# Layer 1 of a CIN network as three fp32r terms, with the low parts of the squares on GpSimd, and a rearranged front and last pair

## The chip, the cores and the metric

One core of a Trainium2 chip. The metric is the device time of one execution in microseconds (us). Each timed run gives one time; the kernel before took 430.91 us in the median of three (430.17 to 431.34).

## The reference

The model is an xDeepFM recommender with a batch of 512, 26 features, an embedding width of 32 and 13 dense values, all in float32:

```
emb  = tables[feature, sparse]                        # 512 x 26 x 32
for w, b in ((conv1_w, conv1_b), (conv2_w, conv2_b)): # two CIN layers
    hp = einsum('bhd,bmd->bhmd', xk, x0)              # x0 = emb; xk = emb, then 64 rows of layer 1
    xn = sigmoid(einsum('oi,bid->bod', w, hp) + b)    # 128 outputs
    xk, res = xn[:, :64], res + xn[:, 64:]
cin_out  = sum over the width of res, times cin_w, + cin_b
deep_out = 832+13 -> 1024 -> 512 -> 256 -> 1 with tanh on emb and dense
out = linear(sparse, dense) + cin_out + deep_out + bias   # 512 values
```

## The kernel before

The batch is cut into 16 *pairs* of 32 rows; a pair has two halves c of 16 rows times 32 embedding columns, so 512 columns each. The order of every engine is written out by hand; engines meet at semaphores that only count up.

**Layer 1 by squares.** Since 2ab = (a+b)² - a² - b², the products of all feature pairs come from squares. TensorE adds rows in `sums_of` (L396 to L405; `x` is stored as an fp32r high part and an fp32r low part), ScalarE squares the 351 sums into `sq` (`squares`, L562), in 3 tiles of 117, and `layer1` (L407) multiplies them by the weights `w1_sb` in plain fp32: 3 tiles u, two column halves q, so 6 matmuls a half c and 12 a pair. fp32 matmuls appear in the trace as two instructions each. The two column halves run side by side in the array. `sigmoid` (L571) makes `xk` and `res1` of the result.

**Layer 2 by products.** For each of 13 tiles t of a pair VectorE multiplies `xk` by a repeated row of x0 (L730), and `main` (L435) multiplies the product by `w2_sb` in fp32. Seven of the tiles take the repeated row from PSUM, where `spread_tile` (L423) puts it by an fp32r matmul into a ring of three double banks shared with the sums (`slot_free`, L386); six ("copied", tiles 2, 3, 6, 7, 10, 11) take it from SBUF, where SyncE's broadcasts put it (L305, 256 KB each and two a tile). `sigmoid2` (L584) and `fold2_of` end the layer.

**Order in the loop.** TensorE's order in pair i is in L507 to L520: four groups of tiles, before each the sums and spreads listed for it (`SUMS_IN`, `SPREADS_IN`), behind the first two `layer1(i + 1, c)`. VectorE (L716 to L746) runs the 13 products, with `x_low(i + 2)` (L659, two subtractions of 0.68 us) behind t = 5, `fold1_of`, `turn` (a transpose for the deep part), `fold2_of` and `piece_low` (low part of a piece of the weights W1) between. GpSimd issues the gathers of embedding rows (L347), seven a pair, one pair after the other, each when the one before has landed. SyncE lays gathered rows out in HBM (`lay_out`), brings them back (`fetch`, into `raw`) and issues the broadcasts; `fetch(i + 3)` is the last thing of its iteration i, behind six broadcasts that wait for `main_done`. ScalarE rounds `raw` to `x` (`x_high`, L552).

**The deep part.** Three layers with fp32r terms hi·hi, lo·hi and hi·lo (`deep`, L448). W1 comes in 14 pieces, one a pair, which ScalarE and VectorE split; the input `xt` is split in the last pair by ScalarE (L640) and GpSimd (L376), and `deep(0, 0)` stands in the last pair behind tile 7. After layer 0, TensorE adds the dense part (L537) and the CIN sums (L541) into the row of outputs; the last tanh, two fp32 matmuls (L545), one addition on VectorE and one DMA end the kernel.

**The front.** 13 fp32 matmuls (L476) keep TensorE busy until pair 0 has come; then sums, layer 1 and spreads of pair 0. `x_low(1)` stands behind VectorE's second product.

## Time and profile before

| What | Time, us |
|---|---|
| Timed runs, median (lowest to highest) | 430.91 (430.17 to 431.34) |
| The profiled execution, own time | 432.29 |
| Span of its trace | 430.4 |
| TensorE busy | 413.3 |
| VectorE busy | 320.0 |
| GpSimd busy | 167.3 |
| ScalarE busy | 161.0 |

The span runs from the first to the last instruction; what lies outside it, 1.9 us of the profiled execution's own time, is start and end of the launch. Busy times are sums over the span, and matmuls are pipelined: a matmul's own time is longer than the distance to the next one, so costs on TensorE are read from starts. A wait is told with the instruction that ended it.

### The profile page before, as it was taken

How to read it: one execution, taken by the hardware profiler on the slowest of the kernel's cores; microseconds unless marked ns; L12 is line 12 of the kernel's file. 1: busy time of each engine (PE TensorE's matmuls, PEld its weight loads, DVE VectorE, ACT ScalarE, POOL GpSimd, SP SyncE). 2: the span in 40 equal slices, each digit the busy share in tenths (PEclk: the TensorE clock that was granted, in tenths of full speed). 3: DMA queues.
4: the chain of work that ended last, by engine and by line, in shares of the span. 5: the costliest groups of instructions: out<-in, count | busy, mean ns of one | idle time of the engine just before them, and what ended most of it. 6: DMA issues, size and time to landing. Idle time of an engine off the chain costs nothing. (4 is left out here: it accounts for less than half of the span.)

```text
span 430.4 us, 5216 instructions
## 1 busy us (share of the span) xinstructions
PE 413.3 (96%) x1874; PEld 167.6 (39%) x1874; DVE 320.0 (74%) x356; ACT 161.0 (37%) x264; POOL 167.3 (39%) x146
## 2 busy tenths in 40 slices
PE   3978989999999999999999999999999999999997
PEld 1422323333333333333233333333333344886784
DVE  4115799898999799999798998998989895332121
ACT  3073252544544534535253544443543411111011
POOL 6663466664746584675540000000000193870000
PEclk9996999999999999999999999999999999999999
DMA  5357696888786898778887778675856720320000
GB/s 195 82 122 164 168 229 162 194 192 196 177 202 141 200 193 210 173 191 184 191 190 189 178 186 192 163 201 133 213 143 153 177 66 10 114 76 0 0 2 0
DMA packets 38304, 64.03 MB, mean 149 GB/s; under 512 B 19601, under 2 KB 22033, under 8 KB 38278
## 3 DMA queue, kind: packets, MB, share of 16 engines
q1 hardware_dynamic: 34694, 61.93, 58.3%
q0 software_dynamic: 3584, 1.76, 3.3%
q8 instruction: 15, 0.25, 0.2%
q14 instruction: 11, 0.09, 0.1%
HBM read 61.96 MB, written 1.71 MB: 148 GB/s over the span
## 5 line engine op out<-in xcount | busy, mean ns | idle before, releaser
L355 POOL DMA_INDIRECT emb<-in_table,rows x112 | 132.8, 1186 | 86.1 <-DMA emb<-in_table,rows 52.6
L730 DVE TENSOR_TENSOR prod<-ring,xk 128x1024 f32<-128x1024 f32 x112 | 132.7, 1217 | 29.2 <-PE ring L431 14.2
L730 DVE TENSOR_TENSOR copied<-copied,xk 128x1024 f32<-128x1024 f32 x96 | 115.4, 1242 | 0.5
L441 PE MATMUL conv<-prod,w_sb 128*64 128x512 f32 x448 | 112.2, 615 | 0.0
L441 PE MATMUL conv<-copied,w_sb 128*64 128x512 f32 x384 | 91.9, 594 | 1.5 <-DVE copied L730 1.5
L419 PE MATMUL conv<-sq,w_sb 117*64 117x512 f32 x384 | 88.1, 593 | 0.3 <-issue 0.3
L579 ACT ACTIVATE xk<-conv,const_sb 64x512 f32<-64x512 f32 x64 | 43.7, 683 | 97.2 <-PE conv L419 84.1
L376 POOL TENSOR_TENSOR xt_lo<-xt,xt_hi 128x512 fp32r<-128x512 f32 (+1 forms) x7 | 12.8, 1863 | 122.1 <-ACT xt_hi L640 122.1
L568 ACT ACTIVATE sq<-ring 117x512 f32<-117x512 f32 x90 | 48.6, 594 | 29.7 <-PE ring L403 23.5
L441 PEld LDWEIGHTS conv<-copied,w_sb 128*64 128x64 f32 x384 | 26.8, 137 | 57.6 <-issue 45.4
L419 PEld LDWEIGHTS conv<-sq,w_sb 117*64 117x64 f32 x384 | 27.2, 136 | 54.2 <-issue 53.4
L441 PEld LDWEIGHTS conv<-prod,w_sb 128*64 128x64 f32 x448 | 26.7, 137 | 50.1 <-issue 45.7
L431 PE MATMUL ring<-x,sel_sb 58*128 58x512 f32 x224 | 39.4, 414 | 0.7 <-ACT sq L568 0.7
L664 DVE TENSOR_TENSOR x<-raw,x 26x512 fp32r<-26x512 f32 x32 | 21.9, 683 | 23.8 <-ACT x L559 21.4
L559 ACT ACTIVATE x<-raw 96x512 fp32r<-96x512 f32 x16 | 10.1, 631 | 53.5 <-DMA raw<-laid 50.0
L403 PE MATMUL ring<-x,sel_sb 58*117 58x512 f32 x96 | 24.3, 497 | 4.7 <-issue 4.7
L431 PEld LDWEIGHTS ring<-x,sel_sb 58*128 58x128 f32 x224 | 19.6, 185 | 22.1 <-issue 16.6
L403 PEld LDWEIGHTS ring<-x,sel_sb 58*117 58x117 f32 x96 | 9.0, 180 | 43.3 <-issue 39.9
L760 DVE CAST h_hi<-hf 128x512 fp32r<-128x512 f32 x8 | 7.7, 964 | 20.7 <-ACT hf L652 20.6
L581 ACT ACTIVATE res<-conv,const_sb 64x512 f32<-64x512 f32 x32 | 21.9, 685 | 0.8
L589 ACT ACTIVATE res<-conv,const_sb 128x512 f32<-128x512 f32 x16 | 11.1, 691 | 22.1 <-PE conv L441 21.5
L760 DVE CAST xt_hi<-hf 128x512 fp32r<-128x512 f32 x4 | 1.7, 427 | 20.1 <-ACT hf L652 20.1
(76 smaller groups left out, 299.2 us busy)
## 6 DMA issues: line engine op xcount, KB each, us to landing
copied<-laid SPq DMA_DIRECT2D x192, 256.0 KB
wpiece<-in_mlp SPq DMA_DIRECT2D x22, 256.0 KB
emb<-in_table,rows POOLq DMA_INDIRECT x112
raw<-laid SPq DMA_DIRECT2D x32, 52.0 KB
laid<-emb SPq DMA_DIRECT2D x16, 96.0 KB
sel_f<-in_sel SPq DMA_DIRECT2D x1, 832.0 KB, 5.7
const_sb<-in_const SPq DMA_DIRECT2D x1, 626.0 KB, 4.2
w_sb<-in_w SPq DMA_DIRECT2D x1, 416.0 KB, 6.3
```

Of the source, the lines that this page charges most:

```text
L355: pool.indirect_dma_start(out=emb[0:n, i, j, :], out_offset=None, in_=table, in_offset=bass.IndirectOffsetOnAxis(ap=rows[0:n, i, j:j + 1], ...
L376: nc.gpsimd.tensor_tensor(xt_lo[0:n, k, :], xt[0:n, k, :], xt_hi[0:n, k, :].bitcast(F32), ALU.subtract).then_inc(xt_lo_done, 1)
L403: mm = nc.tensor.matmul(sums_bank(i, u)[0:UK, c, :], sel1_sb[at:at + XK, u, :], x[i % RX][at:at + XK, :], start=True, stop=True)
L419: mm = nc.tensor.matmul(l1_bank(i, c)[o, :], w1_sb[:, u, o], sq[i % 2][0:UK, u, c, :], start=(u == 0), stop=(u == UT - 1))
L431: mm = nc.tensor.matmul(spread_bank(r)[:, c, :], sel2_sb[at:at + XK, t, :], x[i % RX][at:at + XK, :], start=True, stop=True)
L441: mm = nc.tensor.matmul(conv[i % 2][c * HALF:(c + 1) * HALF, :], w2_sb[:, t, :], prod_of(r)[:, c, :], start=(t == 0), stop=(t == T2 - 1))
L568: nc.scalar.activation(sq[i % 2][0:UK, u, c, :], sums_bank(i, u)[0:UK, c, :], ACT.Square)\
L579: nc.scalar.activation(xk[i % 2][q * HALF:(q + 1) * HALF, c, :], bank[0:HALF, :], ACT.Sigmoid, bias=small_sb[0:HALF, C_CB1:C_CB1 + 1]).the ...
L581: nc.scalar.activation(res1[i % 2][c * HALF:(c + 1) * HALF, :], bank[HALF:P, :], ACT.Sigmoid, bias=small_sb[HALF:P, C_CB1:C_CB1 + 1]).then ...
L589: nc.scalar.activation(res2[i % 2][:, :], conv[i % 2][:, :], ACT.Sigmoid, bias=small_sb[:, C_CB2:C_CB2 + 1]).then_inc(l2_read, 1)
L664: nc.vector.tensor_tensor(x[i % RX][at + XLO:at + XK, :], raw[i % RX][at:at + M, :], x[i % RX][at:at + M, :].bitcast(F32), ALU.subtract).t ...
L730: nc.vector.tensor_tensor(prod_of(r)[:, :, :].rearrange("p c n -> p (c n)"), left[:, :, :].rearrange("p c n -> p (c n)"), xk[i % 2][:, :, ...
```

## The change

1. **Layer 1** for pairs 2 to 15: ScalarE, behind each two squares, also writes their rounded copies `sq_hi`; the low part `sq - sq_hi` is made per (u, c), five of six on GpSimd (`LOWS`) and (2, 0) on VectorE behind its tile 2. `layer1` issues 18 fp32r matmuls of full width (128 columns) a pair instead of 12 fp32 ones of half width. Pairs 0 and 1 keep fp32.
2. **GpSimd's order**: in pair i it waits for product 4, 8 and 12, does one, two and two low parts, and then three, two and two gathers of pair i + 4. Only the first four pairs are gathered ahead of the loop. `gather(1)` no longer waits for the rows of pair 0.
3. **TensorE's groups** are tiles 0-3, 4-7, 8-10, 11-12. The sums of pair i + 2 now stand behind groups 0 and 1, in front of `layer1(i + 1, c)`, and in front of group 2.
4. **The low part of x**: four fetches a pair instead of two (raw also lands in the rows of the low part), one instruction on VectorE instead of two, behind tile 2 instead of 5. `fetch` stands in front of the fifth broadcast of its iteration, `lay_out` behind the second. `x_high(i + 2)` is the first thing of ScalarE's iteration.
5. **Front**: 12 warm matmuls instead of 13; the dense part's fp32 matmul and a copy on ScalarE stand in pair 0; `x_high(1)` stands ahead of `sigmoid(0, 1)`, `x_low(1)` ahead of the first product.
6. **W1**: the low parts of its last 5 of 7 row tiles are made in the last two pairs, in room that the squares leave (`late_copy`, `late_low`, `late_high`); VectorE splits only 4 pieces in the loop. `xt` is split up to its last 32 columns from pair 14 on, the rest in pair 15. `deep(0, 0)` stands behind tile 10.
7. **End**: the CIN sums are weighed on VectorE and need one fp32 matmul after layer 0; the last tile of the last deep layer, its tanh, the row matmul and the addition are cut in halves of 256 columns.

```diff
-LAY_AT = 3
-DEEP_AT = 1
-GROUPS = ((0, 1, 2, 3), (4, 5, 6, 7), (8, 9, 10, 11), (12,))
+LAY_AT, FETCH_AT = 1, 4
+DEEP_AT = 2
+GROUPS = ((0, 1, 2, 3), (4, 5, 6, 7), (8, 9, 10), (11, 12))
-SUMS_IN = {0: ((1, 2),), 2: ((2, 0),), 3: ((2, 1),)}
+SUMS_BEFORE = {2: ((2, 2),)}
+SUMS_BEHIND = {0: ((2, 0),), 1: ((2, 1),)}
-X_LOW_AT, TURN_AT, FOLD1_AT, PIECE_AT = (10, 5), 9, (5, 7), 11
-WARM = 13
+X_LOW_AT, TURN_AT, FOLD1_AT, PIECE_AT = (10, 2), 9, (5, 5), 11
+KEEP = 2
+LOW_AT, LATE_AT = 2, 10
+WARM = 12
@@ tensor, layer1(i, c) for i >= 2
-                for u in range(UT):
-                    pe.wait_ge(sq_done, squares_up_to(i, u, c))
-                    for q in range(2):
-                        o = slice(q * HALF, (q + 1) * HALF)
-                        mm = nc.tensor.matmul(l1_bank(i, c)[o, :], w1_sb[:, u, o], sq[i % 2][0:UK, u, c, :],
-                                              start=(u == 0), stop=(u == UT - 1))
+                for u in range(UT):
+                    pe.wait_ge(sq_hi_done, highs_up_to(i, u, c))
+                    nc.tensor.matmul(bank[:, :], w1_hi[:, u, :], sq_hi[i % 2][0:UK, u, c, :],
+                                     start=(u == 0), stop=False)
+                    nc.tensor.matmul(bank[:, :], w1_lo[:, u, :], sq_hi[i % 2][0:UK, u, c, :],
+                                     start=False, stop=False)
+                for u in range(UT):
+                    if (u, c) in LOWS:
+                        pe.wait_ge(sq_lo_done, lows_up_to(i, u, c))
+                    else:
+                        pe.wait_ge(sq_lo_dve, i - 1)
+                    mm = nc.tensor.matmul(bank[:, :], w1_hi[:, u, :], sq_lo[i % 2][0:UK, u, c, :],
+                                          start=False, stop=(u == UT - 1))
@@ scalar, squares(i, u)
+                if i >= 2:
+                    for c in range(2):
+                        act.wait_ge(sq_done, squares_up_to(i, u, c))
+                        nc.scalar.activation(sq_hi[i % 2][0:UK, u, c, :], sq[i % 2][0:UK, u, c, :], ACT.Copy)\
+                          .then_inc(sq_hi_done, 1)
@@ gpsimd
+            def sq_low(i, u, c):
+                pool.wait_ge(sq_hi_done, highs_up_to(i, u, c))
+                nc.gpsimd.tensor_tensor(sq_lo[i % 2][0:UK, u, c, :], sq[i % 2][0:UK, u, c, :],
+                                        sq_hi[i % 2][0:UK, u, c, :].bitcast(F32), ALU.subtract)\
+                  .then_inc(sq_lo_done, 1)
...
+            for i in range(GSEM):
+                gather(i)
             for i in range(NPAIR):
-                gather(i)
+                ahead = i + GSEM < NPAIR
+                pool.wait_ge(prod_done, T2 * i + 4)
+                if 2 <= i + 1 < NPAIR:
+                    sq_low(i + 1, 2, 1)
...
+                if ahead:
+                    gather(i + GSEM, range(0, 3))
+                pool.wait_ge(prod_done, T2 * i + 8)
+                if 1 <= i and i + 2 < NPAIR:
+                    sq_low(i + 2, 0, 0)
+                    sq_low(i + 2, 0, 1)
...
+                if ahead:
+                    gather(i + GSEM, range(3, 5))
+                pool.wait_ge(prod_done, T2 * i + 12)
...
+                if i + 2 < NPAIR:
+                    sq_low(i + 2, 1, 0)
+                    sq_low(i + 2, 1, 1)
...
+                if ahead:
+                    gather(i + GSEM, range(5, GJ))
@@ vector, x_low(i)
-                for c in range(2):
-                    at = HALF * c
-                    nc.vector.tensor_tensor(x[i % RX][at + XLO:at + XK, :], raw[i % RX][at:at + M, :],
-                                            x[i % RX][at:at + M, :].bitcast(F32), ALU.subtract).then_inc(x_lo_done, 1)
+                nc.vector.scalar_tensor_tensor(x[i % RX][0:XEND, :], raw[i % RX][0:XEND, :],
+                                               small_sb[0:XEND, C_LOW:C_LOW + 1],
+                                               x[i % RX][0:XEND, :].bitcast(F32),
+                                               ALU.mult, ALU.subtract).then_inc(x_lo_done, 1)
@@ tensor, end of layer 0
-                    nc.tensor.matmul(row_ps[0:1, :], small_sb[:, C_AUX:C_AUX + 1], aux[:, :], start=True, stop=False)
-                    by_c = row_ps[0:1, :].rearrange("p (i c b) -> p c i b", c=2, b=CB)
-                    for k, col in enumerate((C_CIN1, C_CIN2)):
-                        for c in range(2):
-                            nc.tensor.matmul(by_c[:, c], small_sb[:, col + c:col + c + 1],
-                                             fold[:, k, :, :], start=False, stop=False, skip_group_check=True)
+                    pe.wait_ge(cin_step, 2)
+                    nc.tensor.matmul(cin_ps, small_sb[:, C_ONE:C_ONE + 2], fold[:, 0, :, :], start=True, stop=True)\
+                      .then_inc(cin_done, 1)
```

## Rows read from the trace of the kernel before

**Rows 1.** the page: busy us; granted clock in 40 slices, in tenths

```profile
PE 413.3 (96%) x1874; PEld 167.6 (39%) x1874; DVE 320.0 (74%) x356; ACT 161.0 (37%) x264; POOL 167.3 (39%) x146
...
PEclk9996999999999999999999999999999999999999
```

**Rows 2.** a 20 us stretch of the loop: busy by engine

```profile
140.00:160.00 20.00, 20.00 (x98) 6.34 (x96) 17.82 (x20) 9.09 (x15) 13.19 (x11) 1.00 0.91 196
```

**Rows 3.** waits of TensorE: us in total, times, longest

```profile
PE conv L441 <- DVE copied L730: 1.5, 3, 0.7
```

**Rows 4.** timeline of TensorE in the loop: start us, us, what

```profile
63.76 1.89 PE L441 MATMUL conv<-copied,w_sb 128*64 128x512 f32 x8
65.47 2.75 PE L419 MATMUL conv<-sq,w_sb 117*64 117x512 f32 x12
...
205.92 2.75 PE L419 MATMUL conv<-sq,w_sb 117*64 117x512 f32 x12
208.60 0.72 PE L431 MATMUL ring<-x,sel_sb 58*128 58x512 f32 x4
...
326.62 1.89 PE L419 MATMUL conv<-sq,w_sb 117*64 117x512 f32 x8
```

**Rows 5.** the chain that ended last: start us, us, what

```profile
367.29 4.78 PE conv L462 x21
...
395.97 0.95 PE conv L537 x2
396.92 1.73 PE conv L541 x8
...
423.58 2.76 PE ring L462 x12
426.34 1.82 PE conv L545 x4
...
428.18 0.68 DVE row_sb L767
```

**Rows 6.** timeline of one pair: a fetch, its landing, who waits

```profile
201.61 0.91 SPq L294 DMA_DIRECT2D raw<-laid  x2
...
207.99 0.63 ACT L559 ACTIVATE x<-raw 96x512 fp32r<-96x512 f32 x1 [4.65 <-DMA raw<-laid]
...
208.65 1.40 DVE L664 TENSOR_TENSOR x<-raw,x 26x512 fp32r<-26x512 f32 x2 [2.23 <-ACT x L559]
```

**Rows 7.** groups of instructions: busy us, mean ns | idle before, releasers

```profile
L730 DVE TENSOR_TENSOR prod<-ring,xk 128x1024 f32<-128x1024 f32 x112 | 132.7, 1217 | 29.2 <-PE ring L431 14.2 <-ACT xk L579 9.5 <-PE conv L441 2.9
L355 POOL DMA_INDIRECT emb<-in_table,rows x112 | 132.8, 1186 | 86.1 <-DMA emb<-in_table,rows 52.6 <-issue 31.4 <-DVE rows L701 2.1
L664 DVE TENSOR_TENSOR x<-raw,x 26x512 fp32r<-26x512 f32 x32 | 21.9, 683 | 23.8 <-ACT x L559 21.4 <-issue 1.7
L365 POOL TENSOR_TENSOR m_lo<-wpiece,m_hi 128x512 fp32r<-128x512 f32 x10 | 13.2, 1319 | 0.8
```

**Rows 8.** VectorE's products: duration min, median, max ns

```profile
L730 DVE TENSOR_TENSOR prod<-ring,xk x112: 1205/1216/1227, 31.1 to 357.5; 128x1024 f32<-128x1024 f32 x112
L730 DVE TENSOR_TENSOR copied<-copied,xk x96: 1178/1218/2319, 34.9 to 354.8; 128x1024 f32<-128x1024 f32 x96
```

**Rows 9.** timelines of GpSimd and then VectorE in the last pair

```profile
343.23 12.83 POOL L376 TENSOR_TENSOR xt_lo<-xt,xt_hi 128x512 fp32r<-128x512 f32 x7 [122.09 <-ACT xt_hi L640]
...
346.59 3.55 DVE L730 TENSOR_TENSOR copied<-copied,xk 128x1024 f32<-128x1024 f32 x2
```

**Rows 10.** timelines of the first pair, TensorE and then VectorE

```profile
26.83 2.79 PE L419 MATMUL conv<-sq,w_sb 117*64 117x512 f32 x12
34.30 1.40 PE L403 MATMUL ring<-x,sel_sb 58*117 58x512 f32 x2 [4.68 <-issue]
...
38.24 1.97 PE L441 MATMUL conv<-prod,w_sb 128*64 128x512 f32 x4
...
42.26 1.23 DVE L730 TENSOR_TENSOR prod<-ring,xk 128x1024 f32<-128x1024 f32 x1 [5.00 <-PE ring L431]
```

More of the change, by code:

```diff
@@ L38 @@
 GSEM = 4
+XEND = HALF + XK
 RING = 3
@@ L256, in build @@
                     enter(("spread", r))
+                for j, u in sums_of_group(SUMS_BEHIND, i, g):
+                    enter(("sums", j, u))
         def l1_bank(i, c):
@@ L720, in _ @@
                     if t == 0:
+                        if i == 0:
+                            x_low(1)
                         dve.wait_ge(xk_ready, 4 * (i + 1))
```

351 lines of the change are left out of this document (264 added, 87 removed).

## The prediction

> **What bounds the kernel now.** I read the page's totals and clock line first, then one stretch of the loop, the waits of TensorE, its timeline, the chain that ended last, and last the groups and the places where GpSimd meets VectorE. TensorE is busy for 96% of the span at full clock but for the start and a dent early on [rows 1]. In 20 us of the loop it is busy for all 20.00, VectorE for 17.82, GpSimd for 13.19, and the DMA engines for 0.91 of their time [rows 2]. In the whole kernel TensorE waits for VectorE's copied products for 1.5 us [rows 3]. So TensorE's own work sets the pace of the loop, VectorE has 2.2 us of slack in 20, and the DMA engines have not much either. The period is read from TensorE's timeline: the first half of layer 1 of pair 2 starts at 65.47 and that of pair 15 at 326.62 [rows 4], so 261.15 / 13 = 20.09 us a pair. Behind the loop the chain is TensorE alone up to the last 0.68 us on VectorE [rows 5].
>
> **Layer 1 (change 1, on the path).** A half of layer 1 now runs from 205.92 to the next kind of work at 208.60, 2.68 us [rows 4]; two halves make 5.36 us a pair. The trace has no fp32r layer 1, but fp32r matmuls of full width in the deep part: 21 of them in 4.78 us [rows 5], 0.228 us each, partly with 77 rows, so the 117 rows here should cost the same. 18 x 0.228 = 4.10 us. Equal fp32 steps are 0.43 us apart (four from 63.76 to 65.47), so six would be 2.57; the last, into fp32r, is 0.1 us longer. That doesn't go, it moves to the sums in front, and 2 x 0.1 us come back. Saved: 5.36 - 4.10 - 0.20 = 1.06 us a pair, x 14 pairs = 14.8 us. From below: if the weight loads can't all be hidden, nothing is saved; from above, 1.26 x 14 = 17.6 us. I take 14.8, since weight loads of the same size are hidden in those 21.
>
> **ScalarE and VectorE (off the path).** ScalarE gets six copies of 117x512 a pair, by the 0.63 us of its rounding of x [rows 6] 3.8 us; its busy time is 9.09 of 20 us [rows 2], so it goes to about 12.9 in 19. VectorE loses one of two subtractions of 0.68 us in x_low and, from pair 5 on, a piece_low (taken at the same 0.68), and gains one sq_low (0.68): 17.8 - 0.7 = 17.1 us a pair in 19. Both are hidden, VectorE with 1.9 us to spare.
>
> **GpSimd (change 2).** A subtraction takes 1.32 us there (L365), a gather 1.19 us and 0.3 us to the next (31.4 us of "issue" over some 100 of them) [rows 7]. 5 x 1.32 + 7 x 1.49 = 17.0 us a pair in 19: it fits if nothing holds it. The question is what it does to VectorE. Products that read PSUM take 1.205 to 1.227 us whatever else runs; copied ones, which read SBUF twice, take 1.218 but once 2.319 [rows 8]. That was in the last pair, where GpSimd's seven subtractions took 12.83 us, 1.83 each instead of 1.32, and two copied products 3.55 us instead of 2.35 [rows 9]. So they hold each other up, by 1.1 to 1.2 us at a time for VectorE and 0.5 for GpSimd. The change starts the low parts when product 4, 8 or 12 is done. Behind 4 and 8 stand two products from PSUM (2.3 us), behind 12 three (3.4 us); one low takes 1.3, two take 2.6. The first and third place hold them; the second overlaps by 0.3 us with the transpose and the reduction behind product 9, which read one tile each. I take no collision as the rule. Between that and one collision for each low (5 x 1.17 = 5.9 us on VectorE) lies the range. The gathers fall beside copied products as before, where those kept 1.218 us; I take them at nothing. If they slip, their cover is the pair in which a gather is ahead of its lay_out.
>
> The page "SBUF — State Buffer" of the Trainium skill (section "Who interferes with whom") says that a VectorE instruction with two SBUF inputs shuts out a GpSimd instruction that reads SBUF and the other way round, while one with a single SBUF input does not. The trace agrees, with 2.319 against 1.227 us. By that rule it is the place of each low part that decides, which is my second rival.
>
> **Fetches and order (changes 3, 4).** raw is asked for at 201.61 and has landed at 207.99, and VectorE stands 2.23 us for it [rows 6], though TensorE loses only some tenths by that. The new fetch goes out one group of tiles (about 3.5 us) earlier, but is wanted at tile 2 instead of 5, some 5 us of VectorE's order earlier; four issues instead of two cost SyncE 0.9 us more, beside 12 broadcasts a pair. I cost it at nothing; if it comes late, x_low stops VectorE ahead of product 3. The sums of u = 2 now stand right before the spreads that need their bank: the spread of the next tile 1 waits for ScalarE's two squares, which stand behind three sigmoids. And from that spread to product 3 VectorE has three products, x_low and sq_low (about 3 x 1.14 + 1.3 = 4.7 us, with semaphores 5.2), while TensorE has two mains, the next spreads and three mains (about 5.4 us). That is close; I take 0.2 us a pair as lost, -2.8 us in 14 (bounds: +0.4 a pair, when today's small waits go too, and -1.0). New period: 20.09 - 1.06 + 0.20 = 19.2 us.
>
> **Front (change 5).** Now TensorE stands from about 29.6 to 34.30 (4.68 us idle), its granted clock falls to the 1.2 GHz level (the dent in [rows 1]), one tile of main takes 1.97 us, and VectorE waits 5.00 us for the spread of tile 4, until 42.26 [rows 10]. With x_high(1) and x_low(1) first, the sums of pair 1 can start near 31.5 and product 0 about 0.7 us later than now. If the clock holds at 2.4 GHz, tile 4 starts near 37.5, 4.8 us earlier; if it falls all the same, near 40, 2.5 us earlier. Product 0 can also come 1.5 us late. I take 4.0 us (bounds 1 to 5.5). The dropped warm matmul pays for the moved dense one.
>
> **Last pair and end (changes 6, 7).** In the last pair the same work stands in another order: deep(0, 0) waits for ScalarE's and GpSimd's splits either way and is now covered by fewer mains, but GpSimd has started earlier. 0, bounds -2 and +1.5. Behind layer 0, 0.95 + 1.73 = 2.68 us [rows 5] become one matmul of 256 columns and the steps into it, about 0.75 us: +1.9. The end: 24 matmuls of 256 columns for 12 of 2.76 us [rows 5]; I take +0.4 us for their 24 weight loads (bounds 0 and +2.7, half-width ones no faster than the 0.228 us of whole ones). Halved, the last tanh (some 0.6 us), row matmul (half of 1.82) and addition (0.68) give back about 0.2 + 0.4 + 0.3 = 0.9. Together 1.9 + 0.9 - 0.4 = 2.4 us saved.
>
> The page "TensorE: Matmul & The Clock Gate" of the Trainium skill (section "LDWEIGHTS (loading the stationary operand)") gives a load of 128 columns 128 / 1.2 = 107 ns, as long as 256 columns at full clock. No run here shows such a pair yet. By that page's figure the halves cost nothing and the estimate for the end would be 2.8 us.
>
> **Sum.** 14.8 - 2.8 + 4.0 + 0 + 2.4 = 18.4 us. Against the profiled execution's own 432.29 us: 413.9. The median of the runs shown is 1.4 us lower, so 412.5 us.
>
> **Rivals.**
> 1. *All goes well.* The clock holds in the front, today's waits go, the end saves all: 14 x 0.4 more, 1.5 and 0.5: about 405 us. For it: TensorE's waits are small now. Against it: the close race before product 3. Chance 0.13.
> 2. *VectorE takes over.* With n collisions of 1.17 us a pair its work is 17.1 + 1.17 n. From n = 2 it passes TensorE's 19.0 (19.4, and what the rings add, say 19.8): 14 x 0.6 = 8.4 us back, 421 us. For it: GpSimd's places have 0 to 0.8 us of spare, and a low part that waits for ScalarE's copy starts late. Against it: VectorE's slack of 1.9 us takes one. Chance 0.20.
> 3. *The DMAs come late.* At a share of 0.91 in 20 us the same bytes in 19.2 us make 0.95, and raw's landing (6.4 us) grows. If VectorE stands 0.5 to 1 us a pair for x_low, 7 to 14 us are back: 420 to 427 us. Against it: the share falls to two thirds once gathers are over, and a part of W1's work moves. Chance 0.10.
> 4. *GpSimd falls behind (the other side).* At 1.83 us a low part its pair is 5 x 1.83 + 7 x 1.49 = 19.6 us, over the period; then each place starts late, lows meet copied products again and layer 1 waits for `sq_lo`. With n = 3, VectorE's pair is 20.6 and with 4 it is 21.8: 14 x (20.6 - 19.2) = 20 us and 36 us above the forecast, 432 to 449 us. It is slower than before from n = 3 on. Against it: it needs most places missed, and from pair 12 on there are no gathers. Chance 0.12.
>
> **Chances and range.** The forecast has 0.45. Faster by over 0.3%, about 1.3 us, which is what a measurement of this kernel can tell: the forecast, rivals 1 and 2 and most of 3, 0.86. Within 0.3%: the far end of 3 and the near end of 4, 0.03. Slower: the rest of 4, 0.11. The range that leaves out 2 in 10 goes from 404 to 425 us.
>
> **What would show it.** Starts of layer 1's matmuls 0.228 us apart and a period of 19.2 us between its blocks; all "prod" products at 1.22 us and no copied one near 2.3; GpSimd's low parts at 1.3 us, not 1.8; tile 4 of pair 0 before 40 us and TensorE's clock at full there; TensorE's waits in the loop under 0.3 us a pair. The forecast is wrong if VectorE's copied products lengthen by the dozen, if VectorE waits for x in most pairs, or if TensorE waits for low parts on GpSimd.

## The result: 1.3% slower, where 4% faster was forecast

The changed kernel takes 436.48 us (median of 4 runs, 435.37 to 438.35), the kernel before 431.12 us beside it. The ratio is 1.0133, 95% interval 1.0094 to 1.0172. The forecast was 412.5 us with a range of 404 to 425.

The traces are of one execution each. For the changed kernel that is its fastest, 435.37 us, and for the kernel before one of 432.29: 3.1 us apart, where the medians are 5.4 apart. What follows places the 3.1 (2.8 in their spans); the other 2.3 lie between executions, and no trace shows them.

The page of the changed kernel: busy time by engine, TensorE's granted clock in tenths in 40 slices, then VectorE's two groups of products (busy us, mean ns).

```profile
span 433.2 us, 5332 instructions
PE 410.3 (95%) x1798; PEld 190.8 (44%) x1798; DVE 337.4 (78%) x357; ACT 214.2 (49%) x363; POOL 258.2 (60%) x221
...
PEclk9986996999999999999999999999999999999999
...
L954 DVE TENSOR_TENSOR prod<-ring,xk 128x1024 f32<-128x1024 f32 x112 | 132.4, 1215 | 17.7 <-PE ring L576 16.5
L954 DVE TENSOR_TENSOR copied<-copied,xk 128x1024 f32<-128x1024 f32 x96 | 134.8, 1431 | 0.0
```

TensorE's work fell by only 3.0 us (413.3 in [rows 1]). The clock line has a second dent now (a stretch at 1.2 GHz), in the seventh slice, and the slice ahead of the first is lower too. In the trace the granted clock is at 1.2 GHz from 24.1 to 27.5, from 34.3 to 41.2 and from 68.5 to 75.3 us; before, only from 33.7 to 40.5. Copied products take 1.431 us on average, where their median was 1.218 [rows 8]; the others still take 1.215.

To place the difference I cut every trace at the start of VectorE's first product of a pair. All times are us of the profiled execution. The last columns are the span and the median with its ratio to the kernel before. Dents come on top in some traces: the rest of 91.9 us in e4, e9 and e17 holds one of 3.4 us near the end of the loop. The traced execution of e3 took 437.37 us, 1.9 over its median; that of e11 took 433.66, 2.4 under.

| kernel | first product | pair 0 | pair 1 | pairs 2-14, mean | rest | span | median | ratio |
|---|---|---|---|---|---|---|---|---|
| before | 31.1 | 27.7 | 18.7 | 20.04 | 92.4 | 430.4 | | 1 |
| changed | 34.1 | 24.1 | 27.1 | 19.82 | 90.3 | 433.2 | 436.48 | 1.0133 |
| e1 | 35.0 | 23.3 | 26.6 | 20.59 | 90.7 | 443.2 | 444.19 | 1.0308 |
| e2 | 33.7 | 25.5 | 25.1 | 19.72 | 90.4 | 431.1 | 433.21 | 1.0053 |
| e3 | 34.4 | 23.8 | 26.3 | 20.03 | 90.4 | 435.3 | 435.45 | 1.0106 |
| e4 | 34.2 | 23.2 | 28.4 | 20.03 | 91.9 | 438.1 | 439.08 | 1.0171 |
| e5 | 33.6 | 23.5 | 27.8 | 21.54 | 90.3 | 455.1 | 456.80 | 1.0606 |
| e6 | 31.6 | 26.6 | 24.2 | 19.77 | 90.4 | 429.8 | 432.35 | 1.0043 |
| e7 | 33.7 | 23.8 | 23.0 | 19.75 | 90.3 | 427.5 | 428.76 | 0.9947 |
| e8 | 32.0 | 26.5 | 18.7 | 20.10 | 90.1 | 428.6 | 429.21 | 0.9963 |
| e9 | 31.9 | 26.8 | 26.6 | 19.75 | 91.9 | 433.9 | 434.41 | 1.0045 |
| e10 | 32.1 | 25.2 | 28.5 | 19.68 | 90.3 | 432.0 | 432.50 | 1.0016 |
| e11 | 35.2 | 24.4 | 23.8 | 19.46 | 95.1 | 431.5 | 436.03 | 1.0056 |
| e12 | 30.6 | 26.5 | 20.6 | 20.56 | 92.4 | 437.2 | 439.35 | 1.0169 |
| e13 | 32.7 | 25.6 | 24.4 | 19.71 | 90.3 | 429.3 | 430.80 | 0.9977 |
| e14 | 33.8 | 23.2 | 26.3 | 19.83 | 90.3 | 431.5 | 431.09 | 0.9985 |
| e15 | 34.0 | 23.8 | 23.8 | 19.85 | 90.4 | 430.0 | 432.75 | 1.0024 |
| e16 | 33.8 | 24.3 | 20.9 | 19.67 | 90.3 | 425.0 | 427.47 | 0.9930 |
| e17 | 34.1 | 23.7 | 20.6 | 19.63 | 91.9 | 425.5 | 426.29 | 0.9892 |

The changed kernel against before: front and pair 0 together -0.6 us (+3.0 and -3.6), pair 1 +8.4, pairs 2 to 14 -0.22 each, -2.8 in all, the rest -2.1. That makes +2.9, and the spans differ by 2.8. So two questions stand: why layer 1 gave so little, and what happened in pair 1.

**Layer 1.** TensorE's timeline in the changed kernel (start us, us, what; x8 counts the instructions of a row):

```profile
157.72 1.89 PE L586 MATMUL conv<-copied,w_sb 128*64 128x512 f32 x8
159.53 0.49 PE L529 MATMUL ring<-x,sel_sb 58*117 58x512 f32 x2
159.95 0.50 PE L555 MATMUL conv<-sq_hi,w_hi 117*128 117x512 f32 x1
160.29 0.39 PE L557 MATMUL conv<-sq_hi,w_lo 117*128 117x512 f32 x1
160.51 0.39 PE L555 MATMUL conv<-sq_hi,w_hi 117*128 117x512 f32 x1
...
161.43 0.84 PE L564 MATMUL conv<-sq_lo,w_hi 117*128 117x512 f32 x3
162.20 0.49 PE L529 MATMUL ring<-x,sel_sb 58*117 58x512 f32 x2
162.53 0.63 PE L576 MATMUL ring<-x,sel_sb 58*128 58x512 f32 x4
163.10 1.94 PE L586 MATMUL conv<-prod,w_sb 128*64 128x512 f32 x8
```

Durations overlap, so starts are subtracted. A block is a run of matmuls of one *form*, that is of one type and shape of operands. Inside layer 1 the matmuls are 0.23 us apart, as forecast. The half from 159.95 to 162.20 takes 2.25 us (2.25 or 2.27 in nearly all), not nine steps of 0.228 = 2.05, since its first and its last step take 0.34 and 0.32. The sums in front take 0.42 (159.53 to 159.95), where next to spreads they take 0.33 (162.20 to 162.53). TensorE's period, from a first half of layer 1 to the next, is the same in all pairs of a trace that nothing holds up (10 of 13 before, 7 in the changed kernel, 11 in e1). This undisturbed period is what the rest goes by: 20.01 us before, 19.78 in the changed kernel, 20.69 in e1, 19.78 in e2, 20.69 in e12 and 19.60 in e16.

**Collisions**, that is, a subtraction on GpSimd and a VectorE instruction with two SBUF inputs holding each other up. Timelines of GpSimd, then of VectorE in the same pair:

```profile
154.88 1.30 POOL L419 DMA_INDIRECT emb<-in_table,rows  x1 [2.17 <-DMA emb<-in_table,rows]
156.48 0.94 POOL L419 DMA_INDIRECT emb<-in_table,rows  x1 [0.30 <-issue]
157.73 0.94 POOL L419 DMA_INDIRECT emb<-in_table,rows  x1 [0.30 <-issue]
158.68 2.54 POOL L427 TENSOR_TENSOR sq_lo<-sq,sq_hi 117x512 fp32r<-117x512 f32 x2
...
159.59 3.86 DVE L954 TENSOR_TENSOR copied<-copied,xk 128x1024 f32<-128x1024 f32 x2
```

GpSimd stood 2.17 us for the landing of the pair's rows, ahead of three gathers, so the two low parts meant for the time of products 8 and 9 ran under tile 10: two copied products took 3.86 us instead of 2.35. In pairs 2 to 11 one product each is stretched so, to 2.57 to 3.87 us.

**Pair 1.** VectorE, then TensorE:

```profile
65.46 2.81 DVE L869 SCALAR_TENSOR_TENSOR x<-raw,const_sb,x 122x512 fp32r<-122x512 f32 x1 [3.60 <-ACT x L723]
...
70.06 1.98 PE L586 MATMUL conv<-copied,w_sb 128*64 128x512 f32 x4 [5.51 <-DVE copied L954]
...
73.69 0.63 PE L555 MATMUL conv<-sq_hi,w_hi 117*128 117x512 f32 x1
```

VectorE stands 3.60 us for the x of pair 3, then its x_low takes 2.81 us instead of 0.75. GpSimd had four low parts in a row from 62.77 to 67.71 us, and x_low ended 0.56 us after them. TensorE idles 5.51 us ahead of tile 3. During this wait its granted clock fell, to the 1.2 GHz level from 68.5 to 75.3 us, and layer 1's matmuls take 0.63 us there and not 0.39.

**Front.** The changed kernel, ScalarE, TensorE, then ScalarE again:

```profile
21.41 0.63 ACT L723 ACTIVATE x<-raw 122x512 fp32r<-122x512 f32 x1 [12.41 <-DMA raw<-laid]
...
22.98 0.96 PE L529 MATMUL ring<-x,sel_sb 58*117 58x512 f32 x6 [2.04 <-DVE x L869]
24.25 4.39 PE L549 MATMUL conv<-sq,const_sb 117*64 117x512 f32 x12 [0.31 <-ACT sq L792]
...
29.24 2.80 PE L549 MATMUL conv<-sq,const_sb 117*64 117x512 f32 x12
...
31.98 0.63 ACT L723 ACTIVATE x<-raw 122x512 fp32r<-122x512 f32 x1 [1.14 <-DMA raw<-laid]
32.63 1.39 ACT L748 ACTIVATE xk<-conv,const_sb 64x512 f32<-64x512 f32 x2
```

The same places in the kernel before:

```profile
19.51 0.63 ACT L559 ACTIVATE x<-raw 96x512 fp32r<-96x512 f32 x1 [10.54 <-DMA raw<-laid]
...
23.44 2.80 PE L419 MATMUL conv<-sq,w_sb 117*64 117x512 f32 x12 [0.32 <-issue]
```

Two things make product 0 3.0 us later, and by their times each would nearly do so alone. The sigmoid that it needs stands behind x_high(1), which waits for its raw rows until 31.98. And layer 1 of pair 0 ended at 32.04 us where it ended at 29.62 before: its x came 1.9 us later, TensorE had run out of work 2.04 us before its first sums, and the first half of layer 1 took 4.39 us instead of 2.80 in the dent at 24.1. In e2, with the same front, x came at 20.48 and there was no such dent; product 0 still came only at 33.7, after a wait of 3.14 us for the rows of pair 1. What pair 0 gains (3.6) only pays for the late start. TensorE stood still all the same, and the clock fell to 1.2 GHz at 34.3 us (33.7 before).

**End.** The chain at the end of the changed kernel:

```profile
396.26 4.78 PE ring L609 x21
401.04 0.52 PE ring L700 x2
...
423.56 2.94 PE conv L609 x12
426.50 2.87 PE ring L623 x24
...
430.86 0.78 DVE row_sb L1011 x2
```

The CIN rows take 0.52 us on this chain for 2.68 before [rows 5], and 24 half-width matmuls take 2.87 us, 0.12 each.

### The profile page after: what moved, and what is told of

It is laid out like the page before. It is cut to its first block, busy times and chain, and to the rows that moved or that the text cites. A ratio compares the mean times of both kernels' runs of the same rounds, so it can differ in the third digit from the quotient of the medians.

```text
span 433.2 us, 5332 instructions
## 1 busy us (share of the span) xinstructions
PE 410.3 (95%) x1798; PEld 190.8 (44%) x1798; DVE 337.4 (78%) x357; ACT 214.2 (49%) x363; POOL 258.2 (60%) x221
## 4 chain that ended last, share of the span: by engine, by line
PE 72%; DVE 9%; POOL 6%; DMA 5%; issue 4%; ACT 1%; SPq 1%; DVEq 0%; POOLq 0%
PE conv L586 33%; PE conv L609 8%; PE ring L609 7%; PE ring L576 6%; PE conv L555 5%; DVE copied L954 4%; POOL emb L419 4%; PE conv L557 4%; PE conv L564 4%; PE ring L529 3%; DVE prod L954 3%; DMA emb<-in_table,rows 3%; DMA raw<-laid 2%; PE conv L549 1%; POOL xt_lo L441 1%
## 5 line engine op out<-in xcount | busy, mean ns | idle before, releaser
L419 POOL DMA_INDIRECT emb<-in_table,rows x112 | 133.0, 1187 | 67.7 <-DMA emb<-in_table,rows 39.3
L954 DVE TENSOR_TENSOR copied<-copied,xk 128x1024 f32<-128x1024 f32 x96 | 134.8, 1431 | 0.0
L427 POOL TENSOR_TENSOR sq_lo<-sq,sq_hi 117x512 fp32r<-117x512 f32 x70 | 88.6, 1286 | 40.0 <-DVE copied L954 33.4
L586 PE MATMUL conv<-copied,w_sb 128*64 128x512 f32 x384 | 96.4, 604 | 6.8 <-DVE copied L954 6.7
L737 ACT ACTIVATE sq_hi<-sq 117x512 fp32r<-117x512 f32 x84 | 48.4, 627 | 0.7
L576 PE MATMUL ring<-x,sel_sb 58*128 58x512 f32 x224 | 42.4, 441 | 0.9 <-ACT sq L732 0.9
L555 PE MATMUL conv<-sq_hi,w_hi 117*128 117x512 f32 x84 | 36.8, 438 | 0.0
L869 DVE SCALAR_TENSOR_TENSOR x<-raw,const_sb,x 122x512 fp32r<-122x512 f32 x16 | 14.0, 875 | 25.6 <-ACT x L723 25.6
L557 PE MATMUL conv<-sq_hi,w_lo 117*128 117x512 f32 x84 | 33.5, 399 | 0.0
L529 PE MATMUL ring<-x,sel_sb 58*117 58x512 f32 x96 | 23.8, 498 | 3.5 <-DVE x L869 3.5
L564 PE MATMUL conv<-sq_lo,w_hi 117*128 117x512 f32 x84 | 23.9, 392 | 0.0
L555 PEld LDWEIGHTS conv<-sq_hi,w_hi 117*128 117x128 f32 x84 | 16.1, 192 | 10.6 <-issue 8.1
```

The lines of the kernel that those rows point to most:

```text
L419: pool.indirect_dma_start(out=emb[0:n, i, j, :], out_offset=None, in_=table, in_offset=bass.IndirectOffsetOnAxis(ap=rows[0:n, i, j:j + 1], ...
L427: nc.gpsimd.tensor_tensor(sq_lo[i % 2][0:UK, u, c, :], sq[i % 2][0:UK, u, c, :], sq_hi[i % 2][0:UK, u, c, :].bitcast(F32), ALU.subtract)\
L529: mm = nc.tensor.matmul(sums_bank(i, u)[0:UK, c, :], sel1_sb[at:at + XK, u, :], x[i % RX][at:at + XK, :], start=True, stop=True)
L555: nc.tensor.matmul(bank[:, :], w1_hi[:, u, :], sq_hi[i % 2][0:UK, u, c, :], start=(u == 0), stop=False)
L557: nc.tensor.matmul(bank[:, :], w1_lo[:, u, :], sq_hi[i % 2][0:UK, u, c, :], start=False, stop=False)
L576: mm = nc.tensor.matmul(spread_bank(r)[:, c, :], sel2_sb[at:at + XK, t, :], x[i % RX][at:at + XK, :], start=True, stop=True)
```

## Experiments

**e1: layer 1 in fp32 again, the rest of the change left.**

```
-                if i < 2:          # layer1(): fp32 only for pairs 0, 1
+                if True:           # and no sq_hi, no low parts of squares
```

> The changed kernel with layer 1 in plain fp32 for all pairs: no rounded squares, no low parts, everything else as changed. Theory A: the fp32r layer 1 itself is worth little, since each half costs 2.27 us and the step from the sums into it 0.42 us instead of the 2.05 and 0.23 us forecast, and the low parts stop VectorE in pairs 1 to 11 on top. Then the loop's period goes from 19.8 to about 20.1 us, no copied product is over 1.3 us, pair 1 is 2 us shorter, and the time is 436 to 440 us. Theory B: fp32r saves the 1.06 us a pair of the forecast and the collisions alone hide it. Then the period without it is about 21 us and the time is over 446 us.

Measured: 444.19 us, 1.0308 (1.0286 to 1.0331), between the theories. TensorE's period is 20.69 us in 11 of 13 pairs, without a collision. TensorE's timeline:

```profile
217.11 0.49 PE L518 MATMUL ring<-x,sel_sb 58*117 58x512 f32 x2
217.54 2.80 PE L538 MATMUL conv<-sq,const_sb 117*64 117x512 f32 x12
220.26 0.74 PE L565 MATMUL ring<-x,sel_sb 58*128 58x512 f32 x4
220.93 1.51 PE L575 MATMUL conv<-prod,w_sb 128*64 128x512 f32 x6
```

A lone sums block between mains and layer 1 takes 0.43 us (217.11 to 217.54). So the fp32r layer 1 is worth 0.91 us a pair in the changed order (20.69 against 19.78), and the changed order itself costs 0.68 (20.69 against 20.01 before). Pair 1 stays at 26.6 us with no low part at all: the late x is enough, with the dent of 6.8 us that comes with it.

**e2: gathers behind the low parts.**

```
                 pool.wait_ge(prod_done, T2 * i + 4)
                 if 2 <= i + 1 < NPAIR: sq_low(i + 1, 2, 1)
-                if ahead: gather(i + GSEM, range(0, 3))
                 pool.wait_ge(prod_done, T2 * i + 8)
                 ...                     # both low parts
-                if ahead: gather(i + GSEM, range(3, 5))
+                if ahead: gather(i + GSEM, range(0, 3))
```

> The changed kernel with GpSimd's gathers of a pair moved: none behind product 4, three behind the two low parts of product 8, four behind those of product 12 (before: 3, 2, 2). Theory A: the low parts behind product 8 start 1 to 2 us late because three gathers, the first of which waits for rows to land, stand ahead of them, and so run into the copied product of tile 10. Then tile 10's products fall from 2.6 to 3.9 us to 1.22 in pairs 2 to 11, and TensorE's own 19.4 us sets the period there: 4 to 5 us less, about 432 us. Rival: the low parts wait for ScalarE's rounded squares; then tile 10 is still struck and the time stays at 436 us.

Measured: 433.21 us, 1.0053 (1.002 to 1.0087), 3.3 us under the changed kernel. The stretched products of pairs 2 to 11 are gone, and TensorE's period is 19.78 in all but the first and the last. By the cut that is worth 1.3 us in pairs 2 to 14; pair 1 gives 2.0, pair 0 loses 1.4. So collisions were there, but small, since 19.78 is TensorE's own pace. Of the 3.3 us only these 1.3 are the loop's, where 4 to 5 were expected. Pair 0 lost its 1.4 to the clock at least in part: the dent there lasted 10.2 us and not 6.8.

**e3: front: 14 warm-up matmuls, gathers of pair 1 behind the rows of pair 0.**

> The changed kernel with 14 warm matmuls instead of 12 and the gather of pair 1 waiting for pair 0's rows again. Theory: the first product comes at 34.1 instead of 31.1 us because pair 1's gathers slow the way of pair 0's rows (x arrives 1.9 us later) and TensorE stands 2.04 us ahead of the first sums, after which its clock is at the 1.2 GHz level for 3.4 us and layer 1 of half 0 takes 4.39 instead of 2.8 us. Then the first product starts near 31.5 to 32 us and the time falls by about 2 us, to 434.5. Rival: four fetches instead of two are the delay, then x arrives no earlier and the gain is under 1 us.

Measured: 435.45 us, 1.0106 (1.0085 to 1.0128); first product at 34.4 instead of 34.1. A miss: 31.5 to 32 was expected. Layer 1 of pair 0 now ran at full clock, but x_high(1) waited longer:

```profile
32.34 0.63 ACT L723 ACTIVATE x<-raw 122x512 fp32r<-122x512 f32 x1 [3.58 <-DMA raw<-laid]
...
33.90 0.64 PE L529 MATMUL ring<-x,sel_sb 58*117 58x512 f32 x2 [3.94 <-DVE x L869]
```

**e4: x_low of pair 3 behind tile 5 of pair 1 instead of tile 2.**

> The changed kernel with x_low of pair 3 behind tile 5 of pair 1 instead of tile 2 (as in the kernel before); all other pairs as changed. Theory: in pair 1 VectorE stands 3.60 us for x_high of pair 3, whose fetch lands at 64.8 us, then its own subtraction is held for 2 us by four low parts on GpSimd, TensorE stands 5.5 us for product 3 and falls to the 1.2 GHz level for 6.8 us. Behind tile 5 nothing waits: pair 1 takes 19 to 21 us instead of 27.1, and the time falls by 5 to 7 us, to about 430 us. Rival: the sums of pair 3 behind tile 3 now wait for x_low instead, and TensorE stands as long; then the gain is under 2 us.

Measured: 439.08 us, 1.0171 (1.0132 to 1.021); pair 1 rose to 28.4. VectorE, then GpSimd:

```profile
62.92 4.69 DVE L895 TENSOR_TENSOR sq_lo<-sq,sq_hi 117x512 fp32r<-117x512 f32 x1 [1.76 <-ACT sq_hi L737]
...
62.10 4.95 POOL L427 TENSOR_TENSOR sq_lo<-sq,sq_hi 117x512 fp32r<-117x512 f32 x4
```

VectorE's own low part of 0.68 us now took 4.69: it ended only 0.56 us after the last of four low parts in a row on GpSimd. With the wait for x gone, this alone made tile 3 nearly as late (TensorE idle 4.93 us). The dent behind it lasted 10.2 us here. The idea that the wait was the one cause is refuted; there are two.

**e5: e2 with the sums issued behind layer 1.**

```
-   main(...); sums_of(i + 2, u); layer1(i + 1, c)
+   main(...); layer1(i + 1, c); sums_of(i + 2, u)
```

> As the kernel with the gathers behind the low parts (433.21 us), and the sums of each pair are issued behind the half of layer 1 that they stood before, so that sums and spreads, which have the same form of operands, stand together and TensorE changes its form once less a group. Theory A (TensorE sets the pace of the loop, 19.8 us a pair, and a part of it is paid at each change of form: sums to layer 1 took 0.42 us and a spread alone 0.44, against 0.23 within a form): 19.3 to 19.6 us a pair, time 427 to 431. Theory B (the pace is matmul count alone, or VectorE and ScalarE): 19.8 a pair, 433 to 434; above 434 if the later squares make layer 1 wait.

Measured: 456.80 us, 1.0606 (1.0578 to 1.0633), 21.7 us a pair, worse than either theory. The order of the bank ring is the same, so the second spread now waits for ScalarE's squares of the sums just issued; before, layer 1 covered them:

```profile
169.34 0.49 PE L574 MATMUL ring<-x,sel_sb 58*128 58x512 f32 x2 [0.80 <-ACT sq L730]
...
173.52 0.49 PE L574 MATMUL ring<-x,sel_sb 58*128 58x512 f32 x2 [0.96 <-ACT sq L730]
```

**e6: e2 with the front's order of before.**

```
-            x_high(1); sigmoid(0, 1)        # ScalarE; x_low(1) ahead of product 0
+            sigmoid(0, 1); x_high(1)        # x_low(1) behind product 1; WARM = 14
-                    if j == 0 and i >= 2:   # GpSimd, gather(i) waits for the rows of i - 1
+                    if j == 0 and i >= 1:
```

> As the kernel with the gathers behind the low parts (433.21 us), with the front's order taken back: sigmoid of half 1 of pair 0 ahead of x_high of pair 1, x_low of pair 1 behind product 1, 14 warm-up matmuls, and the gathers of pair 1 waiting for the rows of pair 0. Theory A (the first product waits in the changed kernel for x_high of pair 1, whose raw rows land at 32): first product at 30 to 31.5 us (33.7 in the kernel it starts from), but pair 0 gives about 1.5 of that back, since x_low of pair 1 stands behind product 1 again; time 430 to 432. Theory B (the front is bound by the landing of pair 1's rows in any order): first product plus pair 0 as before, 59 us, time 433.

Measured: 432.35 us, 1.0043 (1.0024 to 1.0063). The first product came at 31.6 (33.7 in e2), pair 0 took 26.6 instead of 25.5, so the two together gave 1.0 us. Their sum is 58.2 us, just as in the changed kernel: the new order of the front shows neither gain nor loss there, and the 1.0 against e2 may be e2's longer dent. The intervals of e2 and e6 overlap.

**e7: e2 with low parts from pair 3 on (layer 1 of pair 2 in fp32) and x_low of pair 3 behind tile 5.**

> As the kernel with the gathers behind the low parts (433.21 us), but layer 1 of pair 2 stays fp32 (no low parts of it, so GpSimd does none in pair 0 and two fewer rows of four in a row at the start of pair 1), and x_low of pair 3 stands behind product 5 of pair 1. Theory A (pair 1 takes 25 to 27 us against 18.7 before because VectorE is held either by x_low of pair 3, whose rows land late, or by the four low parts in a row on GpSimd, and each alone suffices): with both gone pair 1 takes 19.5 to 21, time 427 to 429.5. Theory B (the new order of TensorE in pair 1 is the cause): pair 1 stays at 24 to 26, 432 to 434.

Measured: 428.76 us, 0.9947 (0.9924 to 0.997): this one beats the kernel before. Pair 1 fell from 25.1 to 23.0 and pair 0 to 23.8. What is left in pair 1 is TensorE's wait for x, 1.66 us, and the clock at 1.2 GHz behind it (67.3 to 70.7):

```profile
66.11 0.49 PE L524 MATMUL ring<-x,sel_sb 58*117 58x512 f32 x2 [1.66 <-DVE x L864]
66.53 4.49 PE L544 MATMUL conv<-sq,const_sb 117*64 117x512 f32 x12
```

**e8: the kernel before with the new end alone.**

> The kernel before with the new end alone (one matmul for the CIN rows, last deep tile and row in halves, dense terms at the start); loop and layer 1 untouched. Theory A: the tail behind the first product of pair 15 falls by 2.1 to 2.4 us (92.4 before), nothing else moves; the dense matmul in front costs 0 to 0.5: 428.3 to 429.2. Theory B (the tail is shorter in the changed kernel for its new last pair, the late weights and low parts on GpSimd, and not for the end): 430.5 to 431.5.

Measured: 429.21 us, 0.9963 (0.9946 to 0.998). The rest fell from 92.4 to 90.1 us. The end is worth 2.3 us by itself, as forecast (2.4). The span fell by 1.8, since the pairs 2 to 14 took 0.8 us more in this trace; the median fell by 1.4.

**e9: the repairs of e6 and e7 together, and sums 0 of pair 3 behind group 1 of pair 1.**

> The changed kernel with four repairs together: gathers behind the low parts, the front's order of before (14 warm-up matmuls), low parts from pair 3 on only with x_low of pair 3 behind product 5, and the sums 0 of pair 3 behind group 1 of pair 1 instead of group 0. Theory A (the front and pair 1 lose only by what waits for the raw rows of pairs 1 and 3): first product at 31 to 32 us, pairs 0 and 1 together 45 to 47 (48.8 and 50.6 in the two kernels that had one repair each), pairs 2 to 14 at 19.75; time 423.5 to 426. Theory B (what the late rows cost only moves on to the next wait for x(3)): pairs 0 and 1 together over 48.5, time 427 or more.

Measured: 434.41 us, 1.0045 (1.0018 to 1.0072), a miss: pair 1 took 26.6 us. ScalarE has the squares of pair 3 written ahead of the sigmoid of pair 2, so moving the sums later held the sigmoid up:

```profile
78.11 5.13 PE L546 MATMUL conv<-sq,const_sb 117*64 117x512 f32 x12 [3.96 <-ACT res L747]
```

**e10: e9 with sums 1 of a pair issued with the spreads of group 1.**

```
+                    if g == 1 and i >= 2: sums_of(i + 2, 1)   # behind the spreads
                     for t in tiles_now: main(T2 * i + t)
-                    if g == 1: sums_of(i + 2, 1)
                     layer1(i + 1, L1_IN[g])
```

> As e9_front_and_pair_1, with sums 1 of each pair issued right behind the spreads of group 1, which have their form of operands, and not between the main matmuls and layer 1; no wait is added. Theory A (a change of form between matmuls costs TensorE 0.1 to 0.2 us, and TensorE sets the pace): one block less a pair, 0.1 to 0.35 us a pair less, time 1.5 to 4.5 us under e9. Theory B (changes of form are hidden): same as e9 within 1 us.

Measured: 432.50 us, 1.0016 (0.9991 to 1.0041), 1.9 us under e9. Most pairs take 19.6 instead of 19.8, for one lone block less.

**e11: e2 with layer 1's term of the low weights left out (6 matmuls a half).**

> As the kernel with the gathers behind the low parts (433.21 us, 19.8 us a pair), with the term of the low weights left out of layer 1, 6 of its 9 matmuls a half in place of 9; nothing else. Theory A (TensorE alone sets the pace there): 6 matmuls of 0.23 us less a pair, 18.4 us a pair, time 413 to 416. Theory B (another engine is next to it, with 17.8 us of work of VectorE and its waits for PSUM): 18.8 to 19.5 a pair, time 419 to 430; then the 1.06 us a pair that the prediction took from layer 1 would not have come in full even at its own price.

Measured: 436.03 us. The rest of 95.1 us spoils the total: in the last pair TensorE waited 5.06 us for a low part of xt on GpSimd, and a clock dent of 6.8 us began at 353.6. The loop is what counts. TensorE's period is 19.2 to 20.0 us in 10 of 13 pairs, though it has 1.4 us less to do. Busy time in 20 us of the loop (columns TensorE, weight loads, VectorE, ScalarE, GpSimd, clock, DMA share, GB/s), first e11, then e2:

```profile
140.00:160.00 20.00, 18.83 (x90) 7.04 (x86) 20.00 (x21) 11.80 (x21) 15.84 (x13) 1.00 0.87 201
```

```profile
140.00:160.00 20.00, 20.00 (x93) 8.37 (x92) 18.62 (x22) 12.10 (x22) 15.13 (x13) 1.00 0.81 197
```

VectorE is busy all 20.00 us in e11. Some of that is stretched time: its copied products of tiles 2 and 6 take 1.7 to 2.4 us in pairs 2 to 12, where e2 has none over 1.3. From product to product most pairs have some 18.9 us of VectorE's work, 17.8 in e2. So theory B holds: VectorE with its collisions with GpSimd stands right behind TensorE's 19.78. Whether another place of the low parts would avoid them wasn't tested.

**e12: the kernel before, second spread of groups 0 and 1 issued between the mains.**

```
-   spread a; spread b; main; main; main; main
+   spread a; main; main; spread b; main; main
```

> The kernel before with one thing changed: in groups 0 and 1 of each pair from 1 on the second spread is issued behind two main matmul pairs of the group instead of beside the first spread. The matmuls and their count are the same; TensorE changes its form of operands four times more a pair. Theory A (each change of form costs 0.1 to 0.2 us on TensorE, which sets the pace): 0.3 to 0.6 us a pair more, 4.5 to 9 us in all: 435 to 440. Theory B (free): 430 to 432.

Measured: 439.35 us, 1.0169 (1.0126 to 1.0211). TensorE's period is 20.69 in 12 of 13 pairs for 20.01: +0.68 us for four changes of form more, 0.17 us each. The timeline shows no idle time for it:

```profile
205.75 1.03 PE L441 MATMUL conv<-prod,w_sb 128*64 128x512 f32 x4
206.71 0.49 PE L431 MATMUL ring<-x,sel_sb 58*128 58x512 f32 x2
207.13 1.94 PE L441 MATMUL conv<-copied,w_sb 128*64 128x512 f32 x8
208.90 2.75 PE L419 MATMUL conv<-sq,w_sb 117*64 117x512 f32 x12
```

The two fp32 matmuls of a tile (x4) take 0.96 us (205.75 to 206.71) for 0.43 + 0.43 inside a block, a lone spread 0.42, where two together take 0.65 (208.60 to 209.25 in the kernel before, the first of them in [rows 4]). From mains to fp32 layer 1 (207.13 to 208.90, four steps in 1.77) only the first step, behind the spread, is longer, by 0.05; nothing is lost at the end: both are fp32.

**e13 to e15: pair 1 once more.** e13 is e10 with ScalarE's sigmoids of pair 2 ahead of the squares of pair 3; e15 is e7 with this and with sums 0 of pair 3 behind group 1; e14 is e15 with e10's edit.

> As e10_sums_1_with_spreads (432.5 us; pairs 0 and 1 together 53.7 us), with ScalarE's order in pair 1 set so that the sigmoids of pair 2 stand ahead of the squares of pair 3. Theory A (pair 1 was held by this order alone once x(3) and the low parts were out of the way): pair 1 falls from 28.5 to 19.5 to 21.5, time 424 to 427. Theory B (x(3) is still late for TensorE somewhere): pair 1 over 23, time 428 or more.

> As e7_low_parts_from_pair_3 (428.76 us; first product 33.7, pair 0 23.8, pair 1 23.0), with sums 0 of pair 3 behind group 1 of pair 1, ScalarE's sigmoids of pair 2 ahead of the squares of pair 3, and sums 1 with the spreads of group 1. Theory A: pair 1 falls by 2 to 3.5 us, the pairs 2 to 14 to 19.6, time 422.5 to 425.5. Theory B (the wait only moves): pair 1 stays at 22 to 24, time 426 to 428.

> As e14_pair_1_sums_1, with sums 1 left between the main matmuls and layer 1. Theory A (a change of TensorE's form of operands costs 0.1 to 0.2 us): 19.8 us a pair, time 2 to 3 us above e14. Theory B: same as e14 within 1 us.

Measured: 430.80 (0.9977, 0.9954 to 1.0001), 431.09 (0.9985, 0.9966 to 1.0004) and 432.75 us (1.0024, 1.0 to 1.0048). All three miss their forecasts of pair 1 and of the time. Pair 1 takes 24.4, 26.3 and 23.8 us. The stall had moved to the next ring slot that waits for the squares of pair 3 (here e14):

```profile
81.71 0.50 PE L573 MATMUL ring<-x,sel_sb 58*128 58x512 f32 x2 [2.75 <-ACT sq L733]
```

e14 and e15 also repeat e10's price: 19.6 against 19.8 in the undisturbed pairs, 1.7 us in the medians, a little under the 2 to 3 expected.

**e16: e7 with e10's edit. e17: e16 with the gathers of pair 3 not waiting for the rows of pair 2.**

```
-                    if j == 0 and i >= 2:
+                    if j == 0 and (i == 2 or i >= GSEM):
                         pool.wait_ge(rows_in[(i - 1) % GSEM], ...)
```

> As e7_low_parts_from_pair_3 (428.76 us; pair 1 23.0, pairs 2 to 14 at 19.8), with sums 1 of each pair from 2 on issued right behind the spreads of group 1. Theory A (one block of another form less a pair): 19.6 a pair, 2 to 3 us less, time 425.5 to 427. Theory B: no change, 428.5 to 429.

> As e16_e7_sums_1_with_spreads, but the gathers of pair 3 don't wait for the rows of pair 2 (they start at 35 us and not at 42). Theory A (pair 1 is long because x(3) comes at 65 us): its raw rows land some 5 us earlier, by 60, pair 1 falls from 23 to 19.5 to 21, time 422.5 to 425.5; the rows of pair 2 may land up to 1.5 us later. Theory B (something else in pair 1 is next, or the rows of pair 2 now come too late): pair 1 at 22 or more, time 425.5 to 429.

Measured: e16 427.47 us, 0.993 (0.9899 to 0.9961); e17 426.29 us, 0.9892 (0.9862 to 0.9922). In e17 ScalarE takes up the raw rows of pair 3 at 61.99 us (64.55 in e7, 64.79 in e16), TensorE waits 0.94 us for that x, and pair 1 takes 20.6. ScalarE, VectorE, TensorE:

```profile
61.99 0.63 ACT L722 ACTIVATE x<-raw 122x512 fp32r<-122x512 f32 x1 [1.30 <-DMA raw<-laid]
...
64.86 0.74 DVE L868 SCALAR_TENSOR_TENSOR x<-raw,const_sb,x 122x512 fp32r<-122x512 f32 x1
...
65.75 0.49 PE L524 MATMUL ring<-x,sel_sb 58*117 58x512 f32 x2 [0.94 <-DVE x L868]
```

The control e16 already had 20.9, with x at 64.79 and a wait of 1.25 us, because the clock dent of e7, which had drawn out the layer 1 behind it from 2.80 to 4.49 us, wasn't there. So rows 2.8 us earlier gave 0.3 us in pair 1, not 2, and whether the dent comes is worth 1.7. In e17 the x is there at 62.6 us, but x_low runs in its place behind product 5, at 64.86; this place holds TensorE now and not the rows.

Whether a dent comes also differs between executions of one kernel. The five runs of e16 with a mean granted clock of 0.992 took 424.8 to 426.8 us, the other seven, at 0.988 or 0.984, 425.9 to 430.8. Five of e17's six runs had 0.992 or more. At 0.992 both kernels have a median of 426.3, so e17 is not shown to be faster than e16. It has the lowest median: 1.1% under the kernel before and some 2.4% under the changed one.

## Why the prediction was wrong, step by step

**Layer 1, -14.8 us, is the step that failed most.** The term said 5.36 - 4.10 - 0.20 = 1.06 us a pair. In parts:
- Eighteen fp32r matmuls at 0.228 us each: the distance inside is right (0.23), but a half takes 2.25 to 2.27 us, not 2.05, because its first and last steps take 0.34 and 0.32. That is 0.42 us a pair. The 0.228 came from a chain of 21 matmuls of nearly one form; a block of nine has two ends.
- "That doesn't go, it moves to the sums in front": the prediction saw a change of form once, at 0.1 us, and counted it only at layer 1. The change also takes the sums away from the spreads, where they had shared a block. In one undisturbed pair of each (before and e2) sums and spreads together take 3.09 and 3.50 us, and the mains, which now run into fp32r twice more, 11.56 and 11.76: 0.61 us lost. The step on fetches and order priced only waits. e1 shows it with layer 1 held at fp32 (+0.68), e12 in the kernel before alone (+0.68 for as many changes of form more), and e16 takes one block away and gets 0.18 back.
- So the two blocks of layer 1 save 5.35 - 4.52 = 0.83 us, the other blocks lose 0.61, and 0.22 is left. The period fell by 0.23.

**Extra stalls, +2.8 us.** TensorE's waits in the loop are small, as thought, and the close race ahead of product 3 was won in the loop. What was lost there were collisions: 1.3 us in pairs 2 to 14 (changed against e2).

**No collision as the rule: wrong.** "The first and third place hold them": they do. "The second overlaps by 0.3 us": no, three gathers and a wait for the rows' landing stood ahead of it (39.3 us of such waits on GpSimd in 13 places), so it came late by about a product. The prediction took the gathers at nothing and looked only at where they fall, not at what they wait for. Rival 2 named this mechanism but with two collisions a pair and TensorE already down at 19.0; there was one a pair, worth 0.1 us over TensorE's 19.78.

**ScalarE and VectorE, off the path.** ScalarE went from 9.09 to 12.1 of 20 us, 12.9 forecast; it is off the path. VectorE was to have 1.9 us to spare in 19. Its 17.1 us started from 17.82 busy us in one stretch of 20 us, which isn't a pair; the next two such stretches have 19.06 and 18.40. From product to product a pair has 18.4 us before and 17.8 in e2, so 1.4 us were to spare in 19.2, without collisions. In e11, with TensorE's work down to some 18.4 us, the period stayed between 19.2 and 20.0 in most pairs. So in this order of the engines the forecast 19.2 would at best just have been reached, even at the forecast price of layer 1.

**Pair 1, not in the sum at all, +8.4 us.** The prediction saw that the raw rows are wanted some 5 us earlier and wrote: "if it comes late, x_low stops VectorE ahead of product 3", at nothing. In the loop that held. In pair 1 the rows are still on the start-up chain of gathers, where each pair's wait for the last one's landing. VectorE stood 3.60 us, and four low parts in a row, which only pair 0 sends (those of two places at once), stretched its next instruction by 2.1 us. Each alone suffices (e1: no low parts, 26.6; e4: no wait for x ahead of tile 3, 28.4). A granted clock at 1.2 GHz for 6.8 us (10.2 in e4) came on top. It was priced per pair and never walked through in the pairs that are written out by hand. The traced execution of e16, which had no dent there, gives 6.2 us of it back (27.1 to 20.9).

**Front, -4.0 us.** Product 0 "0.7 us later than now" was 3.0 us later. The raw rows of pair 1 land too late for x_high(1) to stand ahead of the sigmoid, TensorE's clock still fell, and in this execution layer 1 of pair 0 was late as well: "The dropped warm matmul pays for the moved dense one" left TensorE idle for 2.04 us when x came late. The two together gave 0.6. "Product 0 can also come 1.5 us late" was the right place with half the price.

**End, -2.4 us: right.** 2.1 in the changed kernel, 2.3 alone (e8). The CIN term gave 2.68 - 0.52 = 2.16 for the forecast 1.9. Twenty-four half-width matmuls took 2.87 us for 2.76 of the twelve: the low end of the bounds. The page "TensorE: Matmul & The Clock Gate" of the Trainium skill (section "LDWEIGHTS (loading the stationary operand)") gives 107 ns for a load of 128 columns, and the 120 ns from one half-width matmul and its load to the next agree nearly. **Last pair, 0:** the rest column has no room for more than the end gave.

Together: -14.8 + 2.8 - 4.0 - 2.4 = -18.4 forecast; -2.8 (the loop with its stalls), +8.4 (pair 1), -0.6, -2.1 = +2.9 measured. No rival had it: the other-side rival put its loss into every pair, by GpSimd falling behind and TensorE waiting for low parts. GpSimd was late at one of its three places, but TensorE's waits list none for a low part of the squares.

## What to carry to other kernels

Count an engine's changes of form before moving small blocks about: on a saturated TensorE two or three matmuls of another type or shape between long runs cost more than their number, and a price read inside a long run is a lower bound for a short one. When a loop is reordered so that a datum is wanted earlier, walk through the first pairs, with their loads, and not only a pair in the steady state. Where a second engine is within a tenth of the first and can be held up by a third, as VectorE by GpSimd here, a gain on the first can end there. And compare traces at the same granted clock: a dent of 3.4 us was worth 1.7 us, more than several of the edits.
